# Two-tile depthwise blocks and earlier look-ahead in a two-layer convolution kernel on one NeuronCore

## The reference, cut to what matters

```python
def _L0_conv_ref(x, ...):                       # on the group-normalised input
    x1 = gconv3x3(sign(x), w1); x1 = leaky_relu(x1)
    x2 = batchnorm_train(x1, g1, b1)            # mean and variance over all 32 samples
    x3 = batchnorm_train(concat(x2 + xa, xb), g2, b2); x3 = channel_shuffle(x3, 2)
    x4 = batchnorm_train(leaky_relu(gconv3x3(sign(x3), w2)), g3, b3)
    return concat(x4 + x5a, x5b)                # x5a, x5b: halves of x3
def _L1_conv_ref(x, dw_w, ...):                 # deformable 3x3, on the group-normalised input
    value = x @ vp_w.T + vp_b
    om = (depthwise3x3(x, dw_w) + dw_b) @ om_w.T + om_b    # offsets and masks, 8 groups x 9 taps
    ...                                          # bilinear samples of value at the offset places
    return sum_k(mask * sampled) @ op_w.T
x = x + _L0_conv_ref(_gn(x), ...)
x = x + _L1_conv_ref(_gn(x), ...)               # x: 32 x 64 x 56 x 56, float32
```

## Time and profile before

| what | us |
|---|---|
| median of 3 runs (lowest, highest) | 2999.73 (2999.16, 3000.77) |
| the profiled execution's own time | 2998.01 |
| its span, first to last instruction | 2996.1 |
| busy: PE / DVE / ACT / POOL | 2713.6 / 2195.8 / 2107.3 / 1924.4 |
| granted TensorE clock, mean | 0.970 |

### The profile page before, as it was taken

One profiled execution on the slowest core, in us unless ns is written; L12 is line 12 of the kernel. 1 busy time (PEld: TensorE's weight loads), 2 busy tenths in 40 slices (PEclk: granted clock), 3 DMA queues, 4 the chain that ended last, 5 costly groups with the idle time before them and its releaser, 6 DMA issues. The chain is left out here.

```text
span 2996.1 us, 99369 instructions
## 1 busy us (share of the span) xinstructions
PE 2713.6 (91%) x40456; PEld 2166.3 (72%) x40456; DVE 2195.8 (73%) x3108; ACT 2107.3 (70%) x4273; POOL 1924.4 (64%) x1451
## 2 busy tenths in 40 slices
PE   5888859996599999999999999999999999999998
PEld 3555536774388787877878787777778787778786
DVE  4454533334688897989898888989897988889763
ACT  2334326662778787887878787887878787878782
POOL 2000000001788888888988888888888888888892
PEclk9999979998799999999999999999999999999999
DMA  4344459995477777777778786777777787777675
GB/s 109 97 117 108 129 124 264 266 266 158 133 192 205 189 210 194 202 198 193 203 194 215 192 209 184 214 191 200 204 191 199 192 215 189 208 189 210 172 183 153
DMA packets 343609, 558.99 MB, mean 187 GB/s; under 512 B 159184, under 2 KB 245712, under 8 KB 342992
## 3 DMA queue, kind: packets, MB, share of 16 engines
q1 hardware_dynamic: 284112, 461.96, 61.2%
q10 hardware_dynamic: 59136, 91.76, 8.6%
HBM read 351.36 MB, written 202.19 MB: 185 GB/s over the span
## 5 line engine op out<-in xcount | busy, mean ns | idle before, releaser
L1277 PE MATMUL acc_p<-abuf,vbd 128*32 128x170 f32 (+9 forms) x20480 | 1033.4, 370 | 10.7 <-issue 9.6
L1277 PEld LDWEIGHTS acc_p<-abuf,vbd 128*32 128x32 f32 (+1 forms) x20480 | 819.4, 144 | 216.4 <-issue 30.0
L1110 ACT ACTIVATE dwt<-xp,wts 128x224 f32<-128x224 f32 x2016 | 803.1, 488 | 41.0 <-ACT wst L1134 32.3
L981 DVE TENSOR_TENSOR pr<-mh_p,ht 128x864 f32<-128x864 f32 x672 | 669.2, 1052 | 23.2
L243 PE MATMUL cv<-cin,wb 128*64 128x392 bf16 x6912 | 603.1, 338 | 26.0 <-ACT cin L222 26.0
L1254 PE MATMUL win_p<-pr,smat 128*128 128x160 f32 x4032 | 612.0, 306 | 12.6 <-POOL pr L1067 10.9
L1254 PEld LDWEIGHTS win_p<-pr,smat 128*128 128x128 f32 x4032 | 557.6, 191 | 38.5 <-issue 13.3
L243 PEld LDWEIGHTS cv<-cin,wb 128*64 128x64 bf16 x6912 | 409.7, 112 | 213.4 <-ACT cin L222 26.2
L1050 POOL TENSOR_TENSOR dwt<-dwt 128x896 f32<-128x896 f32 x224 | 518.8, 2316 | 4.7 <-ACT dwt L1110 4.7
L1064 POOL TENSOR_TENSOR pr<-pr 128x576 f32<-128x576 f32 x224 | 317.0, 1415 | 211.5 <-DVE pr L981 211.5
L971 DVE TENSOR_TENSOR mh_p<-oms,ht 128x864 f32<-128x864 f32 x224 | 395.3, 1765 | 7.1 <-ACT ht L1125 7.1
(11 more groups left out here) (132 smaller groups left out, 2581.2 us busy)
## 6 DMA issues: line engine op xcount, KB each, us to landing
abuf<-weight_scratch SPq DMA_DIRECT2D x784, 240.0 KB, 4.1
weight_scratch<-wst ACTq DMA_DIRECT2D x112, 800.0 KB, 5.1
xt<-x SPq DMA_DIRECT2D x128, 392.0 KB, 7.6
rows_scratch<-vsb SPq DMA_DIRECT2D x224, 128.0 KB, 3.1
vbd<-rows_scratch SPq DMA_DIRECT2D x896, 32.0 KB, 4.5
x_scratch<-xt SPq DMA_DIRECT2D x64, 392.0 KB, 6.7
y<-x SPq DMA_DIRECT2D x64, 392.0 KB, 5.3
x3h<-x_scratch SPq DMA_DIRECT2D x64, 392.0 KB, 5.7
```

Of the source, the lines that this page charges most:

```text
L981: dve.tensor_tensor(pr[:, j % 2, slots, :, :, :].rearrange("p k e x z -> p e k (x z)"), mh[:, a, :, :].rearrange("p (k x) z -> p k (x z)", ...
L1110: ins = act.activation(dwt[:, j % 2, k, :].rearrange("p (r w) -> p r w", w=W), image[:, r:r + BR, k % 3:k % 3 + W], ACT.Identity, scale=dw ...
L1277: mm = pe.matmul(acc_p[32 * (2 * s + b):32 * (2 * s + b) + 32, 0:2 * TN].rearrange("p (k w) -> p k w", w=W)[:, k0:k1 + 1, x0:x1], vbd[0:K, ...
```

## The change

- First pass: four x buffers instead of three; SP loads x up to four pairs ahead, and loads two more pairs, not one, ahead of the constants. In DVE's step p the group statistics are of pair p + 2 and the channel statistics of pair p + 3, and both come after `leaky` and `moments`; the statistics of pairs 1 and 2 stand in front of the loop. On ACT the next pair's signs, and on PE the group matmul, stand before chunk 1 instead of chunk 2.
- Fold: the two half channels' statistics are folded together; 13 DVE instructions fewer.
- Second pass: x loads one pair further ahead.
- Third pass: `LAG` 4 instead of 5; `half` 0 is applied in step T + 3 (now an odd step), `half` 1 in step T + 4; loads, stores and statistics stand a step sooner, and the image's eight half sums fill steps 0 to 6, with two in step 6 (before: 0 to 3 and 5 to 7, with two in step 7). The depthwise is done for two tiles in nine ACTIVATEs of 448 elements and five POOL additions of 1344, 896, 448, 448 and 448, split over an odd and an even step. POOL's program has no loop.

```diff
-                sp.wait_ge(x_in[0], NX)
-                load_x(sp, 2, x_in[0])
+                for u in range(2):
+                    sp.wait_ge(x_in[u], NX)
+                    load_x(sp, 2 + u, x_in[u])
                 kept.load_constants(sp)
...
-                def step(p, i, u, last):
-                    if not last:
-                        channel_stats(p + 1, i + u, 1 - u)
-                        group_stats(p + 1, 1 - u)
+                def step(p, i, u, groups, stats):
                     leaky(p, u)
                     moments(p, u)
+                    if groups:
+                        group_stats(p + 2, u)
+                    if stats:
+                        channel_stats(p + 3, i + 1 + u, 1 - u)
...
                 kept.make_shifts(dve)
-                with dve.Fori(0, pairs // 2 - 1) as i:
+                channel_stats(1, 0, 1)
+                group_stats(1, 1)
+                channel_stats(2, 1, 0)
+                with dve.Fori(0, pairs // 2 - 2) as i:
...
-                        if c == 2 and not last:
+                        if c == 1 and not last:
                             groups(p + 1)
...
-        LAG = 5
-
-        LOAD_AT = {3: (1, 2), 6: (1, 3), 10: (2, 0), 13: (2, 1)}
+        LAG = 4
+
+        LOAD_AT = {2: (1, 2), 5: (1, 3), 9: (2, 0), 12: (2, 1)}
         HALVES = 2 * PIECES
-        SUM_AT = {0: (0,), 1: (1,), 2: (2,), 3: (3,), 5: (4,), 6: (5,), 7: (6, 7)}
-        STATS_AT, GROUPS_AT = 7, 8
+        SUM_AT = {0: (0,), 1: (1,), 2: (2,), 3: (3,), 4: (4,), 5: (5,), 6: (6, 7)}
+        STATS_AT, GROUPS_AT, DEVIATION_AT = 6, 7, 8
...
-                    n = near(i, j, 4, first, last)
+                    n = near(i, j, 5 if j % 2 else 4, first, last)
                     if n:
-                        depthwise(*n)
+                        (depthwise_first if j % 2 else depthwise_last)((NT * n[0] + n[1]) // 2)
...
                     n = near(i, j, 2, first, last)
                     if n:
                         hats(*n)
+                    if j % 2:
+                        n = near(i, j, 5, first, last)
+                        if n:
+                            taps_three(*n)
                     n = near(i, j, -LAG, first, last)
-                    if n and j % 2:
+                    if n and j % 2 == 0:
                         copy_acc(*n)
                     copy_weights(i, j)
...
-                    n = near(i, j, -5 if j % 2 else -4, first, last)
+                    n = near(i, j, -3 if j % 2 else -4, first, last)
                     if n:
-                        apply(*n, j % 2)
+                        apply(*n, 1 - j % 2)
```

More of the change, by code:

```diff
@@ L323, in _ @@
                         sp.wait_ge(used_ok, 2 * i + u + 1)
[L324 to L327, removed]
+                        load_x(sp, 2 * i + u + 4, x_in[u])
                 for u in range(2):
@@ L330, in _ @@
                     sp.dma_start(lin[:, u, :], l1_d[u, :, :]).then_inc(l1_in[u], 16)
[L331 to L337, removed]
+                for p in range(4):
+                    step(pairs - 4 + p, p % 2)
+                    sp.wait_ge(used_ok, pairs - 3 + p)
+                    wait(sp, x_in2[p % 2], NX * (p // 2))
+                    load_x(sp, p, x_in2[p % 2])
                 for u in range(2):
@@ L492, in _ @@
                 tt(c(EL), c(EL), mv[:, 0, 1:2], ALU.add)
[L493 to L509, removed]
+                cm, ce = st_c[:, :, :, 0], st_c[:, :, :, 1]
+                gm, gr = st_g[:, :, 0, :], st_g[:, :, 2, :]
+                v0, v1 = vv[:, 0, :, :], vv[:, 1, :, :]
+                tt(v0, cm, gm, ALU.subtract)
+                tt(v0, v0, gr, ALU.mult)
+                ts(v1, cm, -2.0, None, ALU.mult)
+                tt(v1, v1, gm, ALU.add)
+                tt(v1, v1, gm, ALU.mult)
+                tt(v1, v1, ce, ALU.add)
+                tt(v1, v1, gr, ALU.mult)
+                tt(v1, v1, gr, ALU.mult)
+                for at, v in ((MA, v0), (EA, v1)):
+                    then(dve.tensor_reduce(sc[:, at:at + 2], v.rearrange("p q t -> p t q"), AX.X, ALU.add))
+                ts(sc[:, MA:MA + 4], sc[:, MA:MA + 4], 1.0 / pairs, None, ALU.mult)
+                tt(v0[:, :, 0], st_x[:, :], st_g[:, :, 2, 0], ALU.mult)
+                then(dve.tensor_reduce(c(ELA), v0[:, :, 0], AX.X, ALU.add))
                 ts(c(ELA), c(ELA), 1.0 / (pairs * HALF), None, ALU.mult)
@@ L1069, in step @@
                 def step(i, j, first, last):
+                    if not last and j == DEVIATION_AT:
+                        deviation(i + 1)
                     n = near(i, j, 1, first, last)
@@ L1072, in step @@
                         merge(*n)
-                    n = near(i, j, 4, first, last)
+                    n = near(i, j, 5 if j % 2 else 4, first, last)
                     if n:
-                        depthwise(*n)
-                    if not last and j == GROUPS_AT:
-                        deviation(i + 1)
+                        (depthwise_first if j % 2 else depthwise_last)((NT * n[0] + n[1]) // 2)
                 pool.memset(abuf[:, :, :], 0.0).then_inc(band_clear, 1)
                 deviation(0)
-                for j in range(4):
-                    depthwise(0, j)
+                for n in range(2):
+                    depthwise_first(n)
+                    depthwise_last(n)
                 merge(0, 0)
-                for j in range(NT):
-                    step(0, j, True, False)
-                with pool.Fori(1, pairs - 1) as i:
+                depthwise_first(2)
+                for i in range(pairs):
                     for j in range(NT):
-                        step(i, j, False, False)
-                for j in range(NT):
-                    step(pairs - 1, j, False, True)
+                        step(i, j, i == 0, i == pairs - 1)
             @block.scalar
@@ L1165, in step @@
                         write_weights(i, j)
-                    n = near(i, j, 5, first, last)
-                    if n:
-                        taps(*n)
-                for j in range(5):
-                    taps(0, j)
-                for j in range(2):
-                    hats(0, j)
+                    if j % 2 == 0:
+                        n = near(i, j, 6, first, last)
+                        if n:
+                            taps_six(*n)
+                for j in (0, 2):
+                    taps_six(0, j)
+                    taps_three(0, j)
+                hats(0, 0)
+                taps_six(0, 4)
+                taps_three(0, 4)
+                hats(0, 1)
                 act.wait_ge(lines_in, 2 * 16)
```

110 lines of the change are left out of this document (62 added, 48 removed).

## The result

| what | before | after |
|---|---|---|
| median of 4 runs (lowest, highest), same chip | 2999.44 (2996.04, 3000.77) | 3038.97 (3031.01, 3047.32) |
| ratio, 95% interval | | 1.0134 (1.0100 to 1.0168) |
| the profiled execution's own time | 2998.01 | 3033.39 |
| its span | 2996.1 | 3031.5 |

The changed kernel is slower by 1.3%. The forecast was 3043 us. Between the two profiled executions the difference is 35.4 us; the forecast had 43.4 for it.

A forecast was written before the change was run, and what follows sets the result against it. PE was taken to set the third pass's pace. First pass -37.3, fold -2.8 and third pass +83.5 gave +43.4 on 2998.0, 3041, plus 1.7 for the median: 3043 us, range 2920 to 3125.

The forecast's parts named there:

- What bounds the kernel: Third pass, 2178 of 2996 us: PE, busy 95%, sets the pace; its idle time is what can be won.
- First pass: First pass: PE's waits for DVE's statistics go, the start gets worse; end at 350.3 instead of 387.6, -37.3 us.
- Fold: Fold between first and second pass: 13 dependent DVE instructions fewer, -2.8 us.
- The way through HBM: Third pass, weights from windows to apply of `half` 0: 11.95 us against PE's 10.8, period 19.75; third pass +83.5 us.
- The double sum: Third pass, DVE's step 6 with two sums: ACT's write of step 7 late by 4 us, 15 x 4 us.
- The sum of the third pass: Windows 1 to windows 223: 111 x 19.75 + 15 x 4 = 2252.3 us, before 2168.8.
- The depthwise blocks: Third pass, ACT and POOL depthwise over two tiles: worth only PE's wait for `dw_ok`, at most 62.7 us.
- The way fits: Rival, third pass: write and reads under 9.8 us, apply of `half` 0 never waits, 2930 us; chance 0.27.
- The write meets other transfers: Rival, third pass: the weights' write takes the median 5.2 us, period 20.75, in all 3144 us; chance 0.12.
- three of four signs: Profile: first pass without `rhs` waits, wait before values gone, about 1 us before each 128-partition apply, long wait once per image.
- The fourth: Third pass, step 9: PE waits about 5 us for the weights' reads once in an image.

The follow-up runs named there:

- Experiment 1: Third pass of the kernel before with the changed kernel's first pass, fold and second pass: 2952.98 us, ratio 0.9852 to the kernel before.
- experiment 6: Changed kernel with the constants loaded before the x of pairs 2 and 3: 3024.92 us.
- Experiment 3: Changed kernel with an idle ACTIVATE of 128x800 and a wait for it ahead of each write of the weights: 3155.51 us.
- experiment 2: Changed kernel, depthwise blocks kept, half columns applied a step later again with the tables of before, next image's first block behind step 9's write: 2972.90 us.
- Experiment 4: Changed kernel with two of the four reads of `half` 0 left out: 2931.54 us.
- 5: Changed kernel with an image's last two sums in steps 6 and 7, statistics and group sums a step later, next image's first block behind step 9's write: 3066.07 us.
- 7: Changed kernel with ACT's three taps of an odd step moved behind the copy and write of the weights: 3057.46 us.
- experiment 8: Changed kernel with copy and write of the weights ahead of both the `hats` and the three taps in ACT's odd step: 3056.40 us.
- experiment 11: Changed kernel with the eighth sum of every image cut to 8 of its 392 columns: 3031.78 us, ratio 1.0136 to the kernel before.
- experiment 10: Changed kernel, constants first, odd-step windows ahead of the apply of `half` 0, ACT's weight copy and write ahead of `hats` and taps: 2977.39 us, ratio 0.9944 to before.
- 12: Third pass of the kernel before, changed first pass, constants loaded before the x of pairs 2 and 3: 2938.85 us, ratio 0.9809 to the kernel before.

## Why the prediction was right

**What bounds the kernel: right.** PE's idle time is what changed, its work did not.

**First pass: right, 2.9 us short** (-40.2 for -37.3). PE resumed at 53.16 where 54.1 was said, mostly because the second pair of x held the constants up by 7.6 us (DVE's first use of them at 46.71, 39.07) and not 8.2; the four chunks behind it took 20.28 us where I had 21.15 from the earlier trace rows. The steps after that cost 18.6 us. Experiment 1 shows that the gain does not depend on the third pass, experiment 6 that with no x ahead of the constants at all the start gains 14 us more. The forecast's 8 us were for one pair ahead of them, as before, and no run has that.

**Fold: right** (-2.7 for -2.8).

**The way through HBM: right, and shown by changing it both ways.** The sum 0.97 + 4.2 + 6.78 = 11.95 came out, with ACT on time, as 0.97 + 4.21 + 0.02 + 7.00 = 12.2 us by the mean parts (12.19 unrounded); the reads are the term that was low, by 0.22. The median write fell from 5.2 to 3.9 us and the mean was 4.21, where I had chosen 4.2 because the write would stand in a gap. Experiment 3 lengthened the way and paid for all of it, experiment 2 gave it two steps and the wait was gone. Experiment 4, the other direction, brought only about half of what the wait promised.

**The double sum: the term was mis-sized.** I had 15 x 4 = 60 us; the write of step 7 was late by 1.67 us in the mean (2.64 against 0.97), 25 us. Over the images with sums the lateness runs from 0.2 to 3.9. The case of the largest is the forecast's own arithmetic, 20.85 us from the start of `copy_om` to the copy of the weights where 20.9 was said:

```profile
1931.03 1.06 DVE L958 TENSOR_TENSOR oms<-om_p,ombt 128x864 f32<-128x864 f32 x1
...
1946.01 1.04 DVE L958 TENSOR_TENSOR oms<-om_p,ombt 128x864 f32<-128x864 f32 x1
```

```profile
1950.21 1.77 ACT L1104 ACTIVATE dwt<-xp,wts 128x448 f32<-128x448 f32 x3
1951.88 0.87 ACT L1150 ACTIVATE wst<-win_p 128x480 f32<-128x480 f32 x2
1952.79 0.37 ACTq L1162 DMA_DIRECT2D weight_scratch<-wst  x1
```

But two things make it the exception. DVE's step with two sums took 14.9 us in every image before; now it takes 13.6 in the mean of 14 images (13.0 to 15.0). And the windows of step 7 come 20.9 us after those of step 5, not 19.75, since the write of step 5 takes 5.0 us; PE's wait for it gives ACT the time that it was short of. Of the forecast's 4.2 that leaves 4.2 - 1.3 - 1.1 = 1.8 us, near the measured 1.67. Two delays that end at the same instruction do not add up; I had taken every period at the mean and put the whole lateness on top.

Taken image by image (DVE's start and step, its copy, the `hats` and the taps, less the time between the two windows), this sum gives the write's issue within 0.03 us in all 14 images, so what makes the write late is shown. How much of DVE's step is the second sum's doing, and that its removal would give 25 us back, is not: no experiment isolated it (5, 7 and 8 moved something else as well, 11 took only 0.66 us out), and in experiment 8, where the write of step 7 is on time, the way from step 7 is 13.68 us instead of 13.85.

**The sum of the third pass** then is 111 x 12.19 + 25 + 111 x 7.78 = 2242 us by the mean parts, measured 2247.2, forecast 2252.3: 27 us too little for the ordinary way and 35 too much for the double sum. That the total came within 5 us owes much to these two cancelling. The 4 us between the two medians are luck in part as well: between the profiled executions the forecast is 8 us off, and the changed kernel's profiled execution lies 5.6 us under its median.

**The depthwise blocks** were costed at the wait for `dw_ok` and nothing else. In the changed kernel that wait is gone from the page, but so it would be behind a longer one. In experiment 2, with the way through HBM covered, they brought no gain: its third pass is 16 us longer than experiment 1's. The three taps ahead of `copy_acc` and the nine taps of step 9 are the likely reasons and were not told apart. This did not matter for the result. POOL's written-out program was not tried by itself.

**The rivals.** "The way fits" did not come true. Its 2930 us stand beside the 2931.5 of experiment 4, but not for its reason: the third pass there is 8 us longer than the rival's, with 96 us of waiting for reads, and the first passes made up for part of it. The period from which it would have decided is 19.36 us; measured were 2247.2 / 111 = 20.2. The rule in the Trainium skill's page "DMA: Bandwidth & Descriptors", section "Anatomy of one DMA — SWDGE (gpsimd) path", gave an estimate of 3.9 us for the write, and the trace's median is 3.9, though the page's fit is for a DMA that GpSimd issues and ACT issues this one; it gave 4.3 us for the reads as one transfer, and the trace has 6.95 for four of them. "The write meets other transfers" did not happen in the mean, but it did in step 5 (5.0 us), and it is what limited experiment 10.

**What would show it:** three of four signs were there (no waits in the first pass but at its start; the wait before the values gone; a wait before each apply of `half` 0, 1.0 to 1.7 us in the mean in the ordinary steps). The fourth, a wait of about 5 us in step 9, was there at half its size: 2.3 us, hardly above the 2.15 of step 7, which comes from the slow write of step 5. That is the double sum's term again.

## What to carry to other kernels

When a result goes out to HBM and comes back before the next one may be made, add up its way from a quiet place in the trace and compare it with what the waiting engine has to do meanwhile; a step taken from the distance between write and use is paid for at every turn once the way is longer than the work left. Read the price of a late engine from several images, not one, and ask what else ends at the same instruction before adding it. And a removed wait is worth only the distance to the next late engine: halving the reads took 2.35 us out of them and gained 0.90.

## What the hardware showed that I had not expected

**A VectorE instruction beside a GpSimd one.** In experiment 11 the second part of a sum on 8 columns took 1.06 us; the shortest of its kind, with no POOL instruction beside it, took 0.225. It ended when POOL's addition, begun 0.10 us before it, ended (1934.97):

```profile
1933.94 1.06 DVE L923 SCALAR_TENSOR_TENSOR y<-l2h,ab,y 128x8 f32 x1
```

```profile
1933.84 1.13 POOL L1056 TENSOR_TENSOR dwt<-dwt 128x448 f32<-128x448 f32 x1
```

The same holds in all 15 images in which the addition stands beside it: 1.05 to 1.12 us, ended 0.02 to 0.03 us behind POOL's. The Trainium skill, page "SBUF — State Buffer", section "SBUF: two separate sides", says that a VectorE operation with two SBUF inputs and a GpSimd operation that reads SBUF exclude each other for a whole instruction; the rows agree in that the VectorE one, begun second, never ended first. It is also a reason to expect that a DVE step changes its length when POOL's instructions change theirs, as the 14.9 and 13.6 us above did; that this is why was not tested.

**The landing of one DMA, from 3.7 to 10.1 us.** The same 800 KB write takes 3.9 us in the median of the changed kernel, 5.2 in the kernel before and 6.8 in experiment 10. What is under way beside it goes with that: in the changed kernel's step 3 other reads are in flight for 1.6 us during a write and it lands after 4.1, in the same step of experiment 10 for 28 us, and it lands after 6.6 (sums over the reads, several at once). That makes the order of the queues part of the price of each move here, and may be why the changed kernel's runs spread over 16 us while those of experiments 1, 2 and 12, which wait for no such transfer, lie within 2 to 3 us.
